# A reordered tile middle, a reordered start and an interleaved last feed-forward in an RWKV-6 block with a ternary feed-forward

## The reference

```python
xx = x_prev - x                                   # x shifted by one token, minus x
mix = tanh((x + xx * time_maa_x) @ maa_w1)        # five small mixes of rank 32
mw, mk, mv, mr, mg = einsum('btfe,fec->fbtc', mix, maa_w2)
xk = x + xx * (time_maa_k + mk)                   # and likewise xw, xv, xr, xg
r, k, v = xr @ Wr.T, xk @ Wk.T, xv @ Wv.T
g = silu(xg @ Wg.T)
decay = exp(-exp(time_decay + tanh(xw @ td_w1) @ td_w2))
# per head of 32: y = r (S + u k v^T);  S = decay * S + k v^T, over all 2048 tokens
y = groupnorm(y) * ln_g + ln_b
x = layernorm(x + (y * g) @ Wo.T)
gamma = mean(|W|) + 1e-6                          # for W_fc and for W_proj
Wq = sign(W) * min(round(|W| / gamma), 1)         # -1, 0 or 1
h = layernorm(gelu(x @ Wq_fc.T)) * w + b
x = layernorm(x + h @ Wq_proj.T)
```

## Time and profile before

| | us |
|---|---|
| median of 3 runs (lowest, highest) | 3052.81 (3050.32, 3054.34) |
| the profiled execution | 3053.38 |
| its span | 3051.6 |
| PE busy | 2890.4 (95%) |
| DVE busy | 2488.5 (82%) |
| ACT busy | 1927.5 (63%) |
| POOL busy | 934.2 (31%) |

### The profile page before, as it was taken

How to read it: one execution, slowest core, us unless ns; L and a number is a source line. 1 busy time by engine, 2 the same in 40 slices (tenths; PEclk the granted TensorE clock), 3 DMA queues, 4 the chain that set the end, 5 groups by cost and what they waited for, 6 DMA issues and landing times.

```text
span 3051.6 us, 101627 instructions
## 1 busy us (share of the span) xinstructions
PE 2890.4 (95%) x40249; PEld 2119.1 (69%) x40249; DVE 2488.5 (82%) x5437; ACT 1927.5 (63%) x4079; POOL 934.2 (31%) x790
## 2 busy tenths in 40 slices
PE   3899999999999999999999999999999999999997
PEld 2576767777767777767777767777767777767775
DVE  6778888878888878888778888778888778888777
ACT  1466666666666666666666666666667666667664
POOL 3223332233332233332233332233332233332232
PEclk8899999999999999999999999999999999999999
DMA  6000000000000000000000000000000000000000
GB/s 217 15 16 16 23 12 23 19 23 16 23 12 23 19 23 16 23 12 23 19 23 16 23 12 23 19 23 16 23 13 23 19 23 16 23 13 23 19 23 15
DMA packets 22523, 73.40 MB, mean 24 GB/s; under 512 B 2805, under 2 KB 3061, under 8 KB 20469
## 3 DMA queue, kind: packets, MB, share of 16 engines
q1 hardware_dynamic: 22132, 67.10, 6.6%
HBM read 50.31 MB, written 16.78 MB: 22 GB/s over the span
## 4 chain that ended last, share of the span: by engine, by line
PE 65%; DVE 21%; issue 9%; ACT 2%; SPq 1%; DMA 1%; DVEq 1%; ACTq 0%; POOLq 0%; POOL 0%
PE psP L408 18%; PE psF L661 11%; PE psP L634 7%; PE psP L450 7%; PE psF L680 4%; DVE HLO L1394 4%; PE psY L532 2%; DVE ARENA L1267 2%; PE psY L548 2%; DVE SUMS L1386 2%; DVE ARENA L1131 2%; DVE ARENA L1205 1%; DVE ARENA L1331 1%; PE psW L489 1%; DVE ARENA L1119 1%
## 5 line engine op out<-in xcount | busy, mean ns | idle before, releaser
L408 PE MATMUL psP<-ARENA,WALL 128*128 128x256 f32 x3072 | 698.6, 382 | 4.9 <-ACT ARENA L752 2.7
L710 ACT ACTIVATE ARENA<-ARENA 32x512 f32<-32x512 f32 (+3 forms) x930 | 523.8, 563 | 201.2 <-DVE ARENA L1205 96.1
L408 PEld LDWEIGHTS psP<-ARENA,WALL 128*128 128x128 f32 x3072 | 577.7, 191 | 83.3 <-POOL ARENA L933 4.2
L1394 DVE SCALAR_TENSOR_TENSOR HLO<-GG,FWB,HHI 128x128 f16<-128x128 f32 x1024 | 347.6, 400 | 283.5 <-ACT HHI L882 278.5
L661 PE MATMUL psF<-XHI,WFC 128*128 128x128 f16 x4096 | 487.9, 220 | 2.2 <-DVE ST L1410 1.9
L661 PE MATMUL psF<-XLO,WFC 128*128 128x128 f16 x4096 | 486.3, 219 | 0.0
L916 POOL TENSOR_TENSOR MT<-ARENA 32x256 fp32r<-32x256 f32 x330 | 319.2, 967 | 439.7 <-ACT ARENA L710 411.0
L933 POOL TENSOR_TENSOR ARENA<-ARENA,XT 128x1024 f32<-128x1024 f32 x128 | 279.5, 2183 | 512.7 <-DVE ARENA L1131 512.7
L661 PEld LDWEIGHTS psF<-XHI,WFC 128*128 128x128 f16 x4096 | 397.8, 98 | 41.0 <-issue 32.9
L661 PEld LDWEIGHTS psF<-XLO,WFC 128*128 128x128 f16 x4096 | 401.8, 98 | 17.6 <-issue 10.3
L680 PE MATMUL psF<-WPJ,HHI 128*128 128x512 f16 x1024 | 389.6, 380 | 13.8 <-ACT GG L873 13.8
(11 more groups left out here) (166 smaller groups left out, 5226.8 us busy)
## 6 DMA issues: line engine op xcount, KB each, us to landing
XT<-x_ch SPq DMA_DIRECT2D x33, 520.0 KB, 3.4
ARENA<-x_tok SPq DMA_DIRECT2D x32, 512.0 KB, 5.0
out<-OUT SPq DMA_DIRECT2D x64, 256.0 KB, 2.1
WALL<-w_all SPq DMA_DIRECT2D x5, 1024.0 KB, 16.5
ARENA<-wfc SPq DMA_DIRECT2D x4, 1024.0 KB, 8.0
ARENA<-wpj SPq DMA_DIRECT2D x3, 1024.0 KB, 25.5
GG<-wpj SPq DMA_DIRECT2D x1, 1024.0 KB, 24.4
OUT<-w2a SPq DMA_DIRECT2D x2, 256.0 KB
```

What stands on the lines that cost most here:

```text
L408: mm = pe.matmul(psP[:, P.bank(f"{name}{g}"), COLS * c:COLS * (c + 1)], WALL[:, w, k, 128 * (2 * g + c):128 * (2 * g + c + 1)], cc(XF[slot ...
L710: return act.activation(o, i, ACT.Copy)
L1394: e = dve.scalar_tensor_tensor(out=HLO[:, k, :], in0=GG[:, u % 2, 0, 128 * m:128 * (m + 1)], scalar=FWB[:, 0, k:k + 1], in1=HHI[:, k, :], ...
```

## The change

Six things are edited. (1) Start: SP issues the small tensors first (first tile, `w1`, `w2`, the decay weights), waits for `mixing_in`, and then issues W_k, the four pieces of W_fc, W_v, W_r, three pieces of W_proj, W_g, waits for the split of `w2`, and issues the last piece and W_o; each projection weight has its own semaphore, and PE waits for it where it first uses it. (2) W_fc too is summed and quantised inside tile 0; the magnitudes of W_proj are summed on ACT (eight Abs activations between the copies of K and of V); quantising W_proj is spread over tile 0, three of its four pieces after L1233; the eight groups of `against_second` move with it, two of them behind the output projection. (3) POOL in every tile: L960 comes before `scale_root`. (4) DVE in every tile: `product` and the outputs of half 1 come before `differences`, `up(1, 0)` before `normed`. (5) The product of gate and LN_B (L1318, four instructions on DVE) becomes one tensor_tensor on POOL behind `out_root`. SP loads XTOK after `kv1` instead of after `kt1`. (6) The last feed-forward: group 1 of `up` goes to banks of its own and is interleaved with `down` of group 0.

```diff
 # SP
+            sp.wait_ge(mixing_in, 16 * NMIXING)
+            weight(W_K)
             for k in range(4):
-                sp.dma_start(RAW[4 + k], wpj[:, 2048 * k:2048 * (k + 1)]).then_inc(raw_in[4 + k], 16)
+                sp.dma_start(FIRST_RAW[k], wfc[:, 2048 * k:2048 * (k + 1)]).then_inc(first_in[k], 16)
+            weight(W_V)
+            weight(W_R)
+            for k in range(3):
+                second(k)
+            weight(W_G)
+            sp.wait_ge(w2_split, 6)
+            second(3)
+            weight(W_O)
...
-                sp.wait_ge(x_full, X.full(it, "kt1"))
+                sp.wait_ge(x_full, X.full(it, "kv1"))
 # ACT, between the copies of K and of V in tile 0
+            def second_magnitudes():
+                act.wait_ge(first_quantised, 1)
+                for k in range(4):
+                    act.wait_ge(second_in[k], 16)
+                    for h in range(2):
+                        if k or h:
+                            act.wait_ge(magnitudes_taken, 2 * k + h)
+                        act.activation(psF[:, :, :].rearrange("p i n -> p (i n)"), SECOND_RAW[k][:, 1024 * h:1024 * (h + 1)], ACT.Abs,
+                                       accum_out=MAGNITUDES[:, 2 * k + h:2 * k + h + 1]).then_inc(magnitudes_taken, 1)
 # PE in tile 0
+                if first:
+                    first_magnitude()       # waits for DVE's total; before the K projection
...
+                if first:
+                    second_magnitude()      # before mix mg and the R projection
...
-                    if first:
-                        against_second(0, i)
+                    if first and i < 2:
+                        against_second(i, 0)
...
                 if first:
-                    against_second(1, 2)
+                    against_second(0, 1)
+                    against_second(1, 1)
...                                         # (0, 2), (1, 2) before z_ready; (0, 3), (1, 3) after wo
 # POOL
+                    if f == 3 and first:
+                        pool.wait_ge(first_quantised, 3)
+                        pool.memset(ARENA1[:, 0:6144], 0.0).then_inc(su_pool, 1)
...
                 if ffn:
                     ffn.bias()
-                    ffn.finish()
...
                 pool.wait_ge(ab_rest, it + 1)
+                if ffn:
+                    ffn.finish()
...
                 if ffn:
                     ffn.normed()
+                pool.wait_ge(y_weighed, it + 1)
+                pool.tensor_tensor(G.rearrange("p (c t) -> p c t", c=KC), G.rearrange("p (c t) -> p c t", c=KC),
+                                   PAR[:, :, LN_B:LN_B + 1].broadcast_to([128, KC, COLS]), ALU.mult).then_inc(y_affine, 1)
 # DVE in tile 0
+                if first:
+                    first_magnitudes((2, 3), 7)
+                    thresholds(0, psF[:, 1, 0:1], 7)
+                    centred_values()
...
                 totals()
+                if first:
+                    quantise_first(0)
                 mix(it, 3, "mr", "k1")
                 if first:
+                    quantise_first(1)
+                    quantise_first(2)
+                    second_total()
...
                 if first:
+                    quantise_first(3)
+                    thresholds(1, psF[:, 0, 0:1], 15)
+                    quantise_second(0)
 # DVE in every tile
+                if ffn:
+                    ffn.finish()
+                outputs(1)
                 dve.wait_ge(m_dve, M.read(it, "mg1"))
                 differences(it + 1)
-                if ffn:
-                    ffn.finish()
-                outputs(1)
-                if ffn:
+                if first:
+                    quantise_second(1)
+                if ffn:
+                    ffn.up(1, 0)
                     ffn.normed()
-                if ffn:
-                    ffn.up(1, 0)
...
-                dve.wait_ge(y_weighed, it + 1)
-                for k in range(KC):
-                    dve.tensor_scalar(cc(G, k), cc(G, k), PAR[:, k, LN_B:LN_B + 1], None, ALU.mult).then_inc(y_affine, 1)
 # PE, the last feed-forward
+                    for g in range(4):
+                        up(0, g)
+                    ...
+                    for g in range(4):
+                        hidden(LAST_UP[g], 1, g).then_inc(last_up, 1)
+                        down(j, 0, g)
+                    stats(j, 0)
+                    ...
+                    for g in range(4):
+                        pe.wait_ge(hlo_ready, 8 * j + 4 + g + 1)
+                        mm = projected(LAST_PRODUCT[:, :], g)
 # DVE, the last feed-forward
+                    for g in range(4):
+                        up(0, g)
+                    fold(j, 0)
+                    for g in range(4):
+                        up(1, g)
+                    moments(j, 0)
+                    fold(j, 1)
+                    product(j, 0)
+                    normed(j, 0)
+                    stored(j, 0)
+                    moments(j, 1, last=True)
+                    product(j, 1, last=True)
+                    normed(j, 1)
+                    stored(j, 1)
```

More of the change, by code:

```diff
@@ L638, in tile @@
                         mix(it, 0, "mw", wait_free)
+                if first:
+                    against_second(0, 3)
+                    against_second(1, 3)
             def feed_forward(j, before):
@@ L649, in tokens, with hidden, summed, projected @@
                         mm.then_inc(w_full, 1)
+                def hidden(bank, p, g):
+                    for m in range(4):
+                        for k in range(KC):
+                            for part, x in enumerate((XHI, XLO)):
+                                mm = pe.matmul(bank[:, 128 * m:128 * (m + 1)],
+                                               WFC[:, k, 128 * (4 * g + m):128 * (4 * g + m + 1)], x[:, p, k, :],
+                                               start=(k == 0 and part == 0), stop=(k == KC - 1 and part == 1))
+                    return mm
+                def summed(bank):
+                    for i in range(2):
+                        mm = pe.matmul(bank[:, i:i + 1], GR[:, i, :], ONES[:, 0:1], start=True, stop=True)
+                    return mm
+                def projected(bank, part):
+                    for m in range(MH // 4 * part, MH // 4 * (part + 1)):
+                        for h in (HHI, HLO):
+                            mm = pe.matmul(bank, h[:, m, :], WPJ[:, m, :],
+                                           start=(m == 0 and h is HHI), stop=(m == MH - 1 and h is HLO))
+                    return mm
                 def up(p, g):
@@ L657, in up @@
                     F.wait_free(pe, j, name, first)
-                    for m in range(4):
-                        for k in range(KC):
-                            for part, x in enumerate((XHI, XLO)):
-                                mm = pe.matmul(psF[:, F.bank(name), 128 * m:128 * (m + 1)],
-                                               WFC[:, k, 128 * (4 * g + m):128 * (4 * g + m + 1)], x[:, p, k, :],
-                                               start=(k == 0 and part == 0), stop=(k == KC - 1 and part == 1))
-                    mm.then_inc(f_full, 1)
+                    hidden(psF[:, F.bank(name), :], p, g).then_inc(f_full, 1)
                 def stats(j, p):
@@ L668, in stats @@
                     F.wait_free(pe, j, f"st_{p}", first)
-                    for i in range(2):
-                        mm = pe.matmul(psF[:, F.bank(f"st_{p}"), i:i + 1], GR[:, i, :], ONES[:, 0:1], start=True, stop=True)
-                    mm.then_inc(f_full, 1)
+                    summed(psF[:, F.bank(f"st_{p}"), :]).then_inc(f_full, 1)
                 def down(j, p, part):
@@ L677, in down @@
                         F.wait_free(pe, j, f"pj_{p}", first)
-                    for m in range(MH // 4 * part, MH // 4 * (part + 1)):
-                        for h in (HHI, HLO):
-                            mm = pe.matmul(psF[:, F.bank(f"pj_{p}"), :], h[:, m, :], WPJ[:, m, :],
-                                           start=(m == 0 and h is HHI), stop=(m == MH - 1 and h is HLO))
-                    mm.then_inc(f_full if part == 3 else down_step, 1)
+                    projected(psF[:, F.bank(f"pj_{p}"), :], part).then_inc(f_full if part == 3 else down_step, 1)
                 def alone():
@@ L872, in up @@
                         act.wait_ge(sums_added, 3 * (PAIRS * j + p) + (-1, 0, 1, 1)[g])
[L873 removed]
+                    act.activation(GG[:, u % 2, 0, :], bank, ACT.Gelu).then_inc(f_act, 1)
                     act.wait_ge(f_act, 8 * j + u + 1)
```

264 lines of the change are left out of this document (135 added, 129 removed).

## The result

The changed kernel takes 3057.37 us (median of 15 runs, 3055.55 to 3060.08) against 3052.01 (15 runs on the same chip, 3049.26 to 3054.34): ratio 1.0018 [1.0011, 1.0025], slower by 5.4 us. Direction and mechanism are those of the forecast; the size is about a third of it. Its profiled span is 3058.3, against 3051.6; the profiled execution of the changed kernel (3060.08) lies 2.7 above its median.

A forecast was written before the change was run, and what follows sets the result against it. PE's waits were taken to bound repeated tiles, a chain over engines the start and last feed-forward. 3053.4 + 25 - 7 - 3.5 = 3068 us, slower by 0.5%; own range 3053 to 3084, with A 3022 to 3084.

The forecast's parts named there:

- What bounds the kernel: Repeated tiles: only PE's waits count, the largest 42.8 us before the second `from_chunk`; start and last feed-forward: a chain over engines.
- The repeated part: Tiles 1 to 31: the 1.37 wait goes, but DVE's longer chain makes PE wait 2.2 at L368; +0.8 each, +25.
- That the port decides: Middle of each tile: POOL's product and DVE's `mixed_by_x` share a port and exclude one another; DVE stands 1.45.
- rival A: Middle of each tile: the port does not decide; PE gains 0.5 to 0.95 per tile, total 3021; chance 0.22.
- the load of XTOK: Each tile: loaded some 9 us later, first read 10 us after it can have landed; costed at nothing.
- the swap of `normed` and `up(1, 0)`: DVE in each tile: the swap leaves their sum before L1307 as it is; no effect.
- L1318: DVE in each tile: removing its 1.14 is worth nothing, since DVE would wait for HHI in exactly that time.
- the root behind L1022: POOL in each tile: FV's root, moved behind old L960, delays only `product`; costed at nothing, with 0.9 cover.
- Start: Start and tile 0: 17.6 us gained at L1233, 9.6 spent again and 1 for the clock; minus 7.
- Rival B: Start and tile 0: the 17.6 gained at L1233 are not given back; total 3057, no change; chance 0.16.
- End: Last feed-forward: shorter PE waits before `down`, DVE's group 0 end beside the last `down` parts; minus 3.5.
- rival C: Repeated tiles: the clock falls in the new 2.2 gap, each tile losing 1.5 more; total 3115; chance 0.05.

The follow-up runs named there:

- half product: Changed kernel with two of four channel groups of the gate and LN_B product on POOL, the rest on DVE: 3034.81 us, ratio to before 0.9942.
- the best of its corners: Changed kernel with the gate and LN_B product back on DVE and the differences ahead of the outputs of half 1: 3002.43 us, ratio to before 0.9831.

## Why the prediction was right in direction and too large

- **What bounds the kernel**: right. The wait of 42.8 went, and the root was held by the differences (0.55 once they are away, 1.60 again with L960 alone ahead).
- **The repeated part** is the step that was mis-sized: +0.8 per tile, measured +0.47, so +25 in the sum and 14.6 in the traces. This is 10.4 too much; start and end, too favourable by 1.2 and 1.4, hide part of it. The term is the two holds of DVE by POOL: PE's wait in front of L368 was to be about 2.2 and is 1.67, the first `mixed_by_x` 1.9 and is 1.68. The chain from the copy of half 1 to the end of `mixed_by_x` was to be 9.77 and is 9.32 (1508.15 to 1517.47). Of the two holds, the product was put at 2.1, twice L941's 1.05, and takes 1.90: the 1.05 hold a fixed part, as the half product's 1.04 and the whole one's 1.90 show, so doubling was wrong. Its hold of L1198 is 1.20 instead of 1.45; the sum also gave L1198 its whole free 0.48 behind POOL's end, where it ends 0.28 behind it. The hold of the differences by POOL's L1032 is 0.34 instead of 0.45 (1.57 long, not 1.68). The two make 0.36 of the 0.45; the rest was not looked into.
- **That the port decides** (against rival A): right in that the product and `mixed_by_x` exclude one another and that this sets the tile, shown by the run with the product on DVE, the half product, and the product that came later. The tile of 90.7 that A asked for is nearly there with the product on DVE (90.87), and not with it on POOL.
- **Costed at nothing, wrongly**: the load of XTOK. I asked only when XTOK is needed, and not what else its 0.5 MB pass by. Moved, it is worth 0.47 per tile once nothing else stands in its place; in the kernel before, the wait at L548 covered it (late packets in 21 tiles, no stall). With the load left behind `kt1`, the changed kernel might have been slower still; this wasn't tried.
- **Costed at nothing, rightly**: the swap of `normed` and `up(1, 0)` (90.11 without it, 90.14 with it), L1318, and the root behind L1022.
- **Start**: -7 forecast, -5.8 measured. The strips came at 86.31 (85 forecast), and 10.5 instead of 10.6 was given back, but not where I had it: PE waited 5.5 for the second total (8 forecast), 4.9 for the first (3), 4.3 and 2.1 behind the pieces. Rival B is out, since 10.5 of the 16.3 was given back: that its 3057 is the time measured is chance.
- **End**: -3.5 forecast, -2.1 measured. Of DVE's 5.7 for group 0 only 3.1 lie beside PE's last `down` and its sums, which end at 3048.35; the other 2.7 stand in front of the last moments, where the forecast had all of it beside `down`.
- **Clock** (rival C is out): 1.00 in the tile with a wait of 1.67, as it was in the tile before. Right.

Open: why the end takes 62.9 to 63.3 in three of the kernels built from before and 60.98 in before itself, and what decides whether the packet of instructions starts early in the load (17 of 31 tiles) or behind most of it.

## What to carry to other kernels

Work moved from DVE to POOL is not off DVE's path if it lies beside a two-input instruction there: ask which instruction of DVE stands beside it, and price the move as the time from that one's start to POOL's end. Moving the same product by a few microseconds was worth 1.08 of 1.20, and leaving it on DVE, in time in which DVE waits anyway, was better still. When a wait is removed, look for what it covered: here a held root, a bank and a late packet of instructions stood behind one line of "issue" and kept back 1.0 per tile by the traces (91.14 against 90.11), 0.8 by the medians, until each was removed; and a reordering with four parts should be timed part by part, since the best of its corners was 1.7% faster than before and the one chosen 0.2% slower.

## What the runs showed of the hardware that was not expected

- A load of 0.5 MB (3.6 us) delays the packets in which instructions come: one of 16 KB started 2.4 us later, and PE stood in the middle of a row of matmuls, reported as "issue", for 0.2 to 1.0 us in 15 tiles and 0.3 to 0.9 in 20 tiles of another kernel. PE went on 2.2 to 2.4 us after such a packet's start in 34 of these 35.
- The held instruction of DVE ends 0.28 to 0.29 behind the end of POOL's in all five kernels in which the two meet, whether it began 0.5, 0.8 or 1.3 after POOL's; a DVE copy of one fp32 tensor was held as well (2.01 and 2.23 instead of 0.69) and ended 0.55 and 0.56 behind.
- POOL's product, when it was there while DVE's two-input instructions followed one another without a gap, stood 2.0 us, behind instructions that began after it.
- POOL's product by a broadcast takes 1.04 for 128x512 and 1.90 for 128x1024: from these two, 0.18 fixed and 1.72 per 1024.
